# Moving the shared expert's products to other steps of a batch in an attention and mixture-of-experts kernel

## The chip, the cores and the metric

One NeuronCore of a Trainium2 chip (trn2). The metric is the device time of one execution of the kernel, in microseconds (us); smaller is better. The kernel before was timed three times.

## What is computed

The input x has 8 batches of 512 rows of 256 numbers. Cut to what matters:

```
xn = layernorm(x)                                  # over the 256 columns
q, k, v = xn @ qkv_w.T                             # 32 heads of width 8
p = softmax(where(|distance| in window 8, q.k * scale * mask, -inf))
s = (p @ v) @ proj_w.T + proj_b                    # local attention
e, score = argmax(xn @ router_w), sigmoid(max(xn @ router_w))     # one of 8 experts a row
routed = (silu(xs @ gate_w[e]) * (xs @ up_w[e])) @ down_w[e]      # xs = xn * score
shared = (silu(xn @ shared_gate_w) * (xn @ shared_up_w)) @ shared_down_w
out = x + s * silu(routed + shared)
```

## The kernel before, in words

The attention is cut into U = 64 steps of two blocks of 32 query rows, UB = 8 steps to a batch. Each engine has its own program, and each program is a loop `for n in range(LAST + 1)` (67 steps, 0 to 66) in which every other piece of work has been given a step by hand. The functions that say what stands in a step are `jobs_of(n)` (products of TensorE that pass through the psM banks), `silu_at(n)` and `result_at(n)`.

Attention in step n: TensorE makes the scores of n into psS (L939, L943). VectorE scales them into Sx (L719, "weigh") and takes row maxima (L729, "largest"); GpSimd adds the band mask in some steps (L439) and subtracts the maxima (L445); ScalarE takes exp (L508) one step later; VectorE transposes the weights in that step (L751, "flipped"); two steps after the scores TensorE multiplies them with the values into psV (L968, "weighted"), and VectorE divides by the sums (L759, L771) and turns the result (L780). L968 of step n waits for VectorE's division in its step n-1; VectorE's division in step n waits for L968 of step n.

The psM jobs. There are four psM banks; `ORDER` lists all jobs, a job's bank is its place in the list modulo 4, and TensorE waits before a job until the job four places ahead of it has been read out (`bank`, `freed`). The jobs, with their lines on TensorE:

- `q`, `k0` in steps 0 and 4 of a batch and `k1` in steps 1 and 5 (L918, L923), of the next half batch; ScalarE copies them out (L497 for q, L478 for k), into qBD and kBD;
- `tp` (L908, transposes of the rows of the next batch) and `v` (L954, four value and router products at the end of the step), in steps 1 to 7 only; ScalarE copies both out (L478, to xnT and to vS); `v` waits for the copies to xnT;
- `sg`, `su`, `sd`, the shared expert: for a batch `sg, su, sg, su, sd, sd`, in steps 0, 1, 2, 3, 4 and 5. `sg` and `su` are L995, and `sd` L990. After sg ScalarE takes tanh (L524) and VectorE makes ag (L787); after su VectorE makes hTs (L792); sd is copied out by ScalarE (L478);
- `xa`, `xb`, `xc`, the routed experts, in pairs in steps 18 to 39 (L1009, L1018, L1027): the rows are transposed, multiplied by gate and up weights, then by down weights. ScalarE takes a tanh of xb (L538), VectorE gates it (L736, L743, ehT), ScalarE copies xc out (L478 to yb) and stores it;
- `pr`, the output projection (L976), in even steps from 4; VectorE adds the bias (L798).

Around them: VectorE normalises the rows of batch n + 1 in step n (L654) for n below 7, keeps the router's values (L660, `logits`), which waits for the four `v` of the step, and after step 7's chooses experts and ranks rows in steps 7 to 10 (L666 to L710). GpSimd then scatters the 32 row tiles, five to a step from step 10 (L424), each after ScalarE has scaled the tile (L576). When all are in DRAM, SyncE loads expert rows (L361) and weights (L348), and the pairs begin in step 18. From step 40 the results are put together, for 16 groups c of two row tiles: in step `silu_at(c) - 1` GpSimd gathers the routed rows on top of the shared ones (L455), in step `silu_at(c)` ScalarE waits for that DMA and takes tanh (L553, ahead of the step's k, q and shared work on its queue) and VectorE multiplies (L804), and in step `result_at(c)` VectorE makes the product with the attention (L811), which GpSimd adds to the output (L432).

Order within a step where it matters below. TensorE: scores, q/k, tp, xc, xb (first), L968, xb (second), xa (first), the shared product, xa (second), v, pr. VectorE: weigh, largest (after flipped in masked steps), normalise, flipped, division, turn, the shared work, silu, logits, attention, result. ScalarE: exp, silu, q/k copies, tp copies, row scaling, xc, xb, xa, the shared work, xa, v.

```
    if n < U and n % UB < 6 and n != U - 3:
        found.append((("sg", "su", "sg", "su", "sd", "sd")[n % UB], n))
```

Of the kernel before, what the change touches and what calls it, by code (L numbers as in the profile page):

```python
# [16 lines left out]
BATCH, SEQ, C = 8, 512, 256  # L17
# [16 lines left out]
U = NTOK // (2 * QB)  # L34
UB = SEQ // (2 * QB)
# [12 lines left out]
BT = SEQ // P  # L48
# [10 lines left out]
NC = T // CT  # L59
LAST = U + 2  # L60
C_STEP = E0 + NP + 2

C_ID = 0
C_M = C_ID + P
# [49 lines left out]
def pair_at(n, lag):  # L114
    p = n - E0 - lag
    return [i for i in (2 * p, 2 * p + 1) if 0 <= i < NX]


def jobs_of(n):

    if n == -1:
        return [("tp", 0), ("tp", 1), ("q", 0), ("k0", 0), ("k1", 0)] + [("v", t) for t in range(BT)]
    found = []
    h = n // UH + 1
    if h < NH and n % UH == 0:
        found += [("q", h), ("k0", h)]
    if h < NH and n % UH == 1:
        found.append(("k1", h))
    if 1 <= n < BATCH:
        found += [("tp", 2 * n), ("tp", 2 * n + 1)]  # L130
    if n == ROUTE:
        found.append(("cnt", 0))
    found += [("xc", i) for i in pair_at(n, 2)]
    found += [("xb", i) for i in pair_at(n, 1)]
    found += [("xa", i) for i in pair_at(n, 0)[:1]]
    if n < U and n % UB < 6 and n != U - 3:
        found.append((("sg", "su", "sg", "su", "sd", "sd")[n % UB], n))
    if n == U:
        found.append(("sd", U - 3))
    found += [("xa", i) for i in pair_at(n, 0)[1:]]  # L140
    if 1 <= n < BATCH:
        found += [("v", t) for t in range(n * BT, n * BT + BT)]
    if n >= 4 and n % 2 == 0 and (n - 4) // 2 < T:
        found.append(("pr", (n - 4) // 2))
    return found


def silu_at(n):
    last = {NC - 2: U - 1, NC - 1: LAST}
    return [c for c in range(NC) if last.get(c, max(C_STEP + 1 + c * 4 // 3, 2 * BT * (c // 2) + 5 + c % 2)) == n]  # L150


def result_at(n):
    last = {NC - 2: U + 1, NC - 1: LAST + 1}
    return [c for c in range(NC) if last.get(c, max(C_STEP + 2 + c * 4 // 3, 4 * c + 6)) == n]


ORDER = [job for n in range(-1, LAST + 1) for job in jobs_of(n)]
JOB = {job: k for k, job in enumerate(ORDER)}


def build(nc, x, wqkv_d, wproj_d, router_w, gate_w, up_w, down_w, sgate_w, sup_w, sdown_w,
# [3 lines left out]
    with ctx:  # L166
# [100 lines left out]
        def full(eng, job):  # L267
            eng.wait_ge(m_full[JOB[job] % MB], JOB[job] // MB + 1)
            return psM[JOB[job] % MB]
# [30 lines left out]
        def _(sp):  # L300
# [62 lines left out]
            def preset(k):  # L363
                rows = slice(k * NTOK // 8, min((k + 1) * NTOK // 8, NTOK - CT * P))
                sp.dma_start(out[rows, :], x[rows, :]).then_inc(d_pre, 16)

            for n in range(LAST + 1):
                if BATCH < n - 1 < U:
                    spread_v(n - 1)
                if ROUTE <= n < ROUTE + 8:  # L370
                    preset(n - ROUTE)
                if n == C_STEP:
                    full(sp, ("xc", NX - 1))
# [31 lines left out]
        def _(pool):  # L405
# [53 lines left out]
            for n in range(LAST + 1):  # L459
                if n < U:  # L460
                    if masked_late(n):
                        banded(n)
                    subtract(n)
                if n == SENT:
                    pool.wait_ge(s_fill, 16 * 10)
                    pool.wait_ge(r_slot, 1)
                for t in range((n - SENT) * SPS, min((n - SENT + 1) * SPS, T)):
                    if t >= 0:
                        scatter(t)
                for c in silu_at(n + 1):  # L470
                    gather(c)
                for c in result_at(n - 1):
                    add_out(c)

        @block.scalar
        def _(act):
# [101 lines left out]
            for n in range(LAST + 1):  # L578
                if 1 <= n <= U:
                    exps(n - 1)  # L580
                for c in silu_at(n):
                    silu(c)
                for job in jobs_of(n):
                    if job[0] in ("q", "k0", "k1"):
                        qk_out(*job)
                    if job[0] == "tp":
                        rows_of(job[1])
# [15 lines left out]
                for job in jobs_of(n):  # L603
                    if job[0] in ("sg", "sd"):
                        shared(*job)
# [7 lines left out]
        def _(dve):  # L613
# [226 lines left out]
            for n in range(LAST + 1):  # L840
# [34 lines left out]
                for c in silu_at(n):  # L875
                    silu(c)
# [233 lines left out]
```

## Time and profile before

| what | value |
|---|---|
| median of 3 runs | 590.56 us (589.58 to 590.71) |
| the profiled execution | 589.39 us, its span 587.6 us |
| TensorE busy, share of the span | 541.6 us, 92% |
| VectorE | 437.7 us, 74% |
| ScalarE | 240.9 us, 41% |
| GpSimd | 254.1 us, 43% |
| TensorE's mean granted clock | 0.986 of full |

Busy shares are averages over stages in which different engines set the pace. An engine's idle time names in angle brackets who ended it: "[1.07 <-DVE hTs L792]" is 1.07 us of idle time that ended when VectorE's L792 had written hTs. The steps can be told apart in the trace by the first scores (L939 or L943) of each. Names in the rows: PE is TensorE, DVE VectorE, ACT ScalarE, POOL GpSimd, SP SyncE.

### The profile page before, as it was taken

What the parts mean: (1) busy time and instruction counts of PE and PEld (TensorE: products, weight loads), DVE (VectorE), ACT (ScalarE), POOL (GpSimd) and SP (SyncE); (2) the same over time, 40 slices, a digit from 0 to 9 for tenths busy, and PEclk for the clock granted to TensorE, in tenths of its full rate; (3) what the DMA queues carried; (4) which work ended last, traced back from release to release, by engine and by line L of the source; (5) the groups of instructions that cost most, each with busy time, mean ns of one, the idle gap of its engine ahead of it and who ended that gap; (6) DMA issues with size and microseconds to landing.
All of it is one profiled execution on the core that took longest, in us unless ns stands there. A gap on an engine that the chain in (4) does not pass through costs nothing.

```text
span 587.6 us, 10330 instructions
## 1 busy us (share of the span) xinstructions
PE 541.6 (92%) x3302; PEld 468.8 (80%) x3302; DVE 437.7 (74%) x1026; ACT 240.9 (41%) x506; POOL 254.1 (43%) x187
## 2 busy tenths in 40 slices
PE   3979999979988999999999999999999999989872
PEld 2757899758867899988899988899888887868762
DVE  4868668998768556566556656645899999999995
ACT  1562554446652443433443442354434364453120
POOL 5333324148885223322322422222365967877452
PEclk9999999989998999999999999999999999999996
DMA  8725433335525667756566756644233756456323
GB/s 295 235 99 185 138 131 104 94 104 181 162 99 157 209 181 215 219 165 210 170 189 207 209 176 207 205 139 134 57 63 55 108 73 88 73 83 91 56 43 55
DMA packets 106633, 83.17 MB, mean 142 GB/s; under 512 B 42196, under 2 KB 104788, under 8 KB 106452
## 3 DMA queue, kind: packets, MB, share of 16 engines
q1 hardware_dynamic: 90740, 65.07, 37.8%
q0 software_dynamic: 10224, 12.33, 12.6%
q10 hardware_dynamic: 5616, 5.11, 2.5%
q8 instruction: 27, 0.44, 0.3%
q14 instruction: 26, 0.21, 0.1%
HBM read 59.41 MB, written 27.00 MB: 147 GB/s over the span
## 4 chain that ended last, share of the span: by engine, by line
PE 54%; DVE 17%; POOL 11%; issue 5%; DMA 5%; ACT 5%; SPq 1%; ACTq 0%; DVEq 0%
PE psM L1018 11%; PE psV L968 10%; PE psS L943 7%; PE psM L1027 5%; POOL xnT L455 4%; PE psM L995 4%; DMA xnT<-ys_dram,slot 4%; POOL Sx L445 3%; PE psM L954 3%; DVE O L771 3%; PE psM L918 3%; PE psM L990 3%; DVE PTs L751 3%; PE psM L923 2%; PE psM L976 2%
## 5 line engine op out<-in xcount | busy, mean ns | idle before, releaser
L445 POOL TENSOR_TENSOR Sx<-Sx,mx 128x752 f32<-128x752 f32 x64 | 98.9, 1545 | 123.4 <-DVE mx L729 123.0
L968 PE MATMUL psV<-VB,PTs 128*128 128x132 f32 x1024 | 131.2, 280 | 14.8 <-DVE O L771 14.8
L968 PEld LDWEIGHTS psV<-VB,PTs 128*128 128x128 f32 x1024 | 125.3, 190 | 19.9 <-issue 18.6
L439 POOL TENSOR_TENSOR Sx<-Sx,cst 128x752 f32<-128x752 f32 x28 | 47.0, 1678 | 173.2 <-DVE Sx L719 173.2
L943 PE MATMUL psS<-kBD,qBD 128*128 128x188 f32 x512 | 97.8, 323 | 0.2 <-DVE Sx L719 0.2
L943 PEld LDWEIGHTS psS<-kBD,qBD 128*128 128x128 f32 x512 | 84.7, 190 | 9.5 <-issue 2.5
L751 DVE STREAM_TRANSPOSE PTs<-Sx 128x512 f32<-128x512 f32 x128 | 82.8, 685 | 4.2 <-ACT Sx L508 4.1
L719 DVE TENSOR_TENSOR Sx<-psS,cst 128x752 f32<-128x752 f32 x64 | 60.0, 938 | 26.9 <-PE psS L943 26.5
L771 DVE TENSOR_TENSOR O<-psV,rs 32x128 f32<-32x128 f32 x256 | 73.5, 287 | 4.8
L1018 PE MATMUL psM<-xT,EB 128*128 128x128 f32 x624 | 76.5, 276 | 0.2 <-DMA EB<-in_L_ffn_up_w 0.2
L1018 PEld LDWEIGHTS psM<-xT,EB 128*128 128x128 f32 x624 | 73.8, 192 | 2.6 <-ACT qBD L497 1.4
L729 DVE TENSOR_REDUCE mx<-Sx 128x16 f32<-128x752 f32 x64 | 59.6, 931 | 13.0 <-POOL Sx L439 11.8
L508 ACT ACTIVATE Sx<-Sx 128x752 f32<-128x752 f32 x64 | 52.9, 827 | 38.7 <-POOL Sx L445 38.5
L995 PE MATMUL psM<-xnT,wsgu 128*128 128x512 f32 x128 | 61.7, 605 | 2.1 <-DVE ag L787 2.1
L478 ACT ACTIVATE kBD<-psM 32x272 f32<-32x272 f32 x128 | 49.3, 385 | 15.3 <-PE psM L923 14.1
L455 POOL DMA_INDIRECT xnT<-ys_dram,slot x28 | 46.5, 1659 | 9.3 <-issue 6.2
L497 ACT ACTIVATE qBD<-psM,cst 128x512 f32<-128x512 f32 x64 | 38.7, 687 | 22.1 <-PE psM L918 22.1
L538 ACT ACTIVATE et<-psM 128x256 f32<-128x256 f32 x39 | 15.0, 384 | 77.5 <-PE psM L1018 73.9
L736 DVE SCALAR_TENSOR_TENSOR ea<-et,psM 128x256 f32<-128x256 f32 x39 | 16.4, 420 | 37.3 <-ACT et L538 36.2
L995 PEld LDWEIGHTS psM<-xnT,wsgu 128*128 128x128 f32 x128 | 22.6, 196 | 18.5 <-issue 16.2
L1027 PE MATMUL psM<-EB,ehT 128*128 128x256 f32 x156 | 36.9, 379 | 0.0
L976 PE MATMUL psM<-wp,OT 128*128 128x256 f32 x128 | 33.9, 388 | 2.7 <-DVE OT L780 2.0
(111 smaller groups left out, 681.5 us busy)
## 6 DMA issues: line engine op xcount, KB each, us to landing
EB<-in_L_ffn_gate_w SPq DMA_DIRECT2D x39, 256.0 KB, 3.2
EB<-in_L_ffn_up_w SPq DMA_DIRECT2D x39, 256.0 KB, 3.7
EB<-in_L_ffn_down_w SPq DMA_DIRECT2D x39, 256.0 KB, 3.0
VB<-v_dram SPq DMA_DIRECT2D x256, 32.0 KB
stage<-xs_dram SPq DMA_DIRECT2D x39, 128.0 KB, 2.3
ys_dram<-yb ACTq DMA_DIRECT2D x39, 128.0 KB, 3.2
xs_dram<-blank SPq DMA_DIRECT2D x9, 512.0 KB, 3.2
v_dram<-vS SPq DMA_DIRECT2D x8, 512.0 KB, 3.0
```

The lines of the kernel that those rows point to most:

```text
L445: nc.gpsimd.tensor_tensor(s, s, mx[n % 3][:, :].unsqueeze(2).broadcast_to([P, 2 * G, KW]), ALU.subtract).then_inc(a_sub, 1)
L455: pool.indirect_dma_start(shared_rows(c * CT)[:, k, :], None, ys_dram, bass.IndirectOffsetOnAxis(ap=slot[:, t:t + 1], axis=0), compute_op= ...
L508: nc.scalar.activation(s, s, ACT.Exp).then_inc(a_exp, 1)
L719: tt(s, psS[:, :, 0:BW].rearrange("p j (g k) -> p j g k", k=KW), mw.unsqueeze(1).unsqueeze(1).broadcast_to([P, 2, G, KW]), ALU.mult).then_ ...
L729: reduce(mx[n % 3][:, :], Sx[n % 3][:, :, 0:KW], AX, ALU.max).then_inc(a_max, 1)
L751: last = nc.vector.transpose(PTs[n % 2][:, k, :, :, :].rearrange("p j i (r q) -> p (j i r) q", q=QB), Sx[n % 3][:, :, k * QB:(k + 1) * QB])
L771: last = tt(o[rows], v[rows, :, :, HD * h:HD * h + HD], inverse[rows].unsqueeze(3).broadcast_to([QB, KC, 8, HD]), ALU.mult)
L943: last = mm(psS[:, j, i * HS * KW:(i + 1) * HS * KW], qBD[h % 2][:, j, k, :, :].rearrange("p s q -> p (s q)"), kBD[h % 2][:, j, :, k * QB: ...
L968: last = mm(psV[:, j, at:at + HS * VW], PTs[n % 2][:, k, j, i, :], VB[n % 2][:, i, k, :, VW * j:VW * j + VW], start=k == 0, stop=k == 1)
L995: last = mm(ps[:, :], wsgu[:, kc, at:at + P], xnT[:, b, kc, WIN:WIN + SEQ], start=kc == 0, stop=kc == KC - 1)
L1018: last = mm(ps[:, f * P:(f + 1) * P], egu[:, i % 2, kc, f * P:(f + 1) * P], xT[:, i % 2, kc, :], start=kc == 0, stop=kc == KC - 1)
L1027: last = mm(ps[:, 0:C], ehT[:, i % 2, fc, :], edn[:, i % 2, fc, :], start=fc == 0, stop=fc == KC - 1)
```

## The change

The same six products of a batch stand in its steps 1, 2, 3, 5, 6 and 7, in the same order, for batches 0 to 6. In batch 7 all stays. The names of the jobs keep the batch and the place among the six, so all semaphores count as before. In `silu_at` a bound on the step moves by two.

```diff
+SHARED = ("sg", "su", "sg", "su", "sd", "sd")
+SPREAD = (1, 2, 3, 5, 6, 7)
...
-    if n < U and n % UB < 6 and n != U - 3:
-        found.append((("sg", "su", "sg", "su", "sd", "sd")[n % UB], n))
+    b, k = divmod(n, UB)
+    if b < BATCH - 1 and k in SPREAD:
+        k = SPREAD.index(k)
+        found.append((SHARED[k], b * UB + k))
+    if b == BATCH - 1 and k < 5:
+        found.append((SHARED[k], n))
     if n == U:
-        found.append(("sd", U - 3))
+        found.append((SHARED[5], U - 3))
...
-    return [c for c in range(NC) if last.get(c, max(C_STEP + 1 + c * 4 // 3, 2 * BT * (c // 2) + 5 + c % 2)) == n]
+    return [c for c in range(NC) if last.get(c, max(C_STEP + 1 + c * 4 // 3, 2 * BT * (c // 2) + 7 + c % 2)) == n]
```

## Rows read from the trace of the kernel before

**Rows 1.** Windows by stage: start:end, length, then each engine's busy time

```profile
core 0: us, PE busy (x) PEld busy (x) DVE busy (x) ACT busy (x) POOL busy (x), PEclk, DMA share, GB/s
22.09:101.62 79.53, 73.22 (x401) 61.51 (x400) 58.99 (x136) 38.14 (x79) 25.43 (x16) 1.00 0.40 131
127.85:186.62 58.77, 54.34 (x304) 45.00 (x303) 45.95 (x109) 32.44 (x67) 44.57 (x41) 0.97 0.48 149
186.62:425.71 239.09, 238.40 (x1605) 216.74 (x1605) 148.01 (x339) 93.28 (x216) 65.77 (x43) 1.00 0.62 181
425.71:576.28 150.57, 140.22 (x839) 118.28 (x837) 140.41 (x315) 56.48 (x102) 101.69 (x68) 1.00 0.49 73
```

**Rows 2.** Windows of single steps: 2, 4, 5, 6 and 7

```profile
41.44:52.03 10.59, 9.53 (x53) 7.69 (x52) 8.11 (x17) 3.97 (x8) 3.20 (x2) 1.00 0.48 162
62.64:75.47 12.83, 12.83 (x74) 11.46 (x73) 7.60 (x17) 8.47 (x18) 3.20 (x2) 1.00 0.40 134
75.47:85.66 10.19, 10.19 (x61) 9.26 (x60) 7.66 (x16) 4.86 (x11) 3.19 (x2) 1.00 0.47 156
85.66:94.07 8.41, 8.41 (x53) 7.77 (x52) 7.04 (x15) 3.76 (x8) 3.01 (x2) 1.00 0.26 79
94.07:101.62 7.55, 7.55 (x49) 6.92 (x48) 5.60 (x15) 3.09 (x6) 3.30 (x3) 1.00 0.49 158
```

**Rows 3.** Timeline of steps 0 and 1, single engines: start us, us, what

```profile
31.52 1.28 ACT L524 ACT_TABLE_LOAD   x1
32.81 0.60 ACT L524 ACTIVATE tg<-psM 128x512 f32<-128x512 f32 x1
...
33.52 0.69 DVE L787 SCALAR_TENSOR_TENSOR ag<-tg,psM 128x512 f32<-128x512 f32 x1 [2.14 <-ACT tg L524]
...
36.86 2.91 PE L954 MATMUL psM<-wqkv,xnT 128*128 128x264 f32 x12 [0.61 <-ACT xnT L478]
40.45 1.16 PE L954 MATMUL psM<-wqkv,xnT 128*128 128x264 f32 x4 [0.68 <-DVE hTs L792]
```

**Rows 4.** Timeline of step 4: ScalarE's last row copies, TensorE's sd and first v

```profile
69.74 1.09 ACT L478 ACTIVATE xnT<-psM 128x512 f32<-128x512 f32 x2
...
69.28 1.89 PE L990 MATMUL psM<-wsdn,hTs 128*128 128x256 f32 x8
71.00 1.32 PE L954 MATMUL psM<-wqkv,xnT 128*128 128x264 f32 x5
```

**Rows 5.** Timeline, VectorE: it takes step 7's router values

```profile
102.25 0.18 DVE L660 COPY EB<-vS 128x32 f32<-128x32 f32 x1 [1.29 <-ACT vS L478]
```

**Rows 6.** Waits of GpSimd from 127.85 to 178.1: total us, times, longest

```profile
POOL xs_dram L424 <- issue: 6.4, 24, 0.3
```

**Rows 7.** Timeline, TensorE: the first expert product, step 19

```profile
186.62 0.57 PE L1018 MATMUL psM<-xT,EB 128*128 128x128 f32 x3 [0.25 <-DMA EB<-in_L_ffn_up_w]
```

**Rows 8.** Windows of single steps with experts: 24 (sg), 28 (sd), 32 (sg)

```profile
238.55:253.04 14.49, 14.48 (x90) 12.35 (x89) 7.72 (x18) 8.22 (x20) 3.11 (x2) 1.00 0.70 200
286.53:300.75 14.22, 14.22 (x94) 13.08 (x93) 7.09 (x16) 7.63 (x18) 3.11 (x2) 1.00 0.64 181
330.81:345.96 15.15, 14.48 (x90) 12.35 (x89) 7.86 (x18) 8.65 (x20) 3.11 (x2) 1.00 0.72 215
```

**Rows 9.** Waits of VectorE from 427.6 to 576: total us, times, longest

```profile
DVE ag L787 <- ACT tg L524: 0.9, 2, 0.5
DVE xnT L804 <- ACT EB L553: 0.9, 1, 0.9
```

**Rows 10.** Timeline of steps 46 and 49, VectorE and ScalarE

```profile
459.47 0.94 DVE L719 TENSOR_TENSOR Sx<-psS,cst 128x752 f32<-128x752 f32 x1 [0.65 <-PE psS L943]
...
482.15 1.57 ACT L478 ACTIVATE kBD<-psM 32x272 f32<-32x272 f32 x4
...
483.59 0.69 DVE L792 SCALAR_TENSOR_TENSOR hTs<-ag,psM 128x512 f32<-128x512 f32 x1
484.19 0.68 DVE L804 SCALAR_TENSOR_TENSOR xnT<-EB,xnT 128x512 f32<-128x512 f32 x1
```

## The prediction

> **What bounds the kernel now.** I first cut the span into stages, because the 92% of TensorE is an average [rows 1]. From the first expert product to step 41 TensorE is busy 238.40 of 239.09 us: there it is the bound, and a product placed there costs its full time. From step 41 on VectorE is busy 140.41 of 150.57 us, with TensorE at 140.22; the waits tell who sets the pace: after 427.6 VectorE waits 1.8 us for ScalarE [rows 9] and 0.65 us for TensorE [rows 10], and what is left of its 10 idle us lies in pauses too short for the view of waits, between instructions that depend on each other. So VectorE bounds that stage. In between, from 127.85 to 178.1, GpSimd scatters; its pauses are 24 of at most 0.3 us [rows 6], so the scatter runs at its own speed and whatever the others do is hidden. Before that, steps 4 to 7 are TensorE's (busy 12.83 of 12.83, 10.19 of 10.19, 8.41 of 8.41, 7.55 of 7.55), and step 2 is not (9.53 of 10.59) [rows 2]. There TensorE's fourth `v` waits until VectorE has read the shared product out of its bank (the wait of 0.68 us for hTs in step 1 is of this kind [rows 3]).
>
> So the change moves products between stages of different owners. No instruction is added or removed, no DMA moves to another place of a queue, and silu_at returns the same steps: for c = 12 the larger term is 57 against 53 before and 55 now, for c = 13 it is 58 against 54 and 56. Only places count.
>
> **Prices.** A shared product takes TensorE 1.72 us, from the start of sd to that of the next job [rows 4]. Its VectorE part takes 0.60 us, from start to start [rows 10].
>
> **Batch 0.** Step 0 loses its sg. VectorE had waited 2.14 us there for the tanh, which came after a table load of 1.28 us [rows 3]. Now VectorE goes on with step 1 2.7 us earlier (the wait and the product). ScalarE, though, needs the load all the same, now ahead of the first exp; exp, k copies and row copies follow without the tanh's 0.5 us ahead of them, of which exp can use 0.3, since it waits for the subtracted maxima. So the first `v`, which waited for these copies until 36.86, comes 0.3 us earlier. The last `v` waited 0.68 us for hTs and started at 40.45 [rows 3]; ag is ready by then, as VectorE is early. With 3.6 us for four `v` from 36.55 the step ends at 40.15 instead of 41.44: **-1.3 us**.
>
> The row shows that the tanh starts 0.01 us after the load ends. The Trainium skill ("ScalarE: Activation LUTs", "What ACT_TABLE_LOAD costs") says otherwise: 1.28 us for the load and another 1.38 us for a drain. By that rule exp and the copies behind it would come 1.4 us later and this gain would be gone; by the row it stands, and the sum takes the row.
>
> Steps 2 and 3 keep a sg or su, and their 10.6 us. Step 4 loses sd, 1.72 us of a full step. But its `v` need the row copies, which ScalarE ends at 70.83, behind the q and k copies; sd ended, and `v` began, at 71.00 [rows 4]. sd filled a wait: its removal gives **0.0** (-0.1 to 0; with the wait gone it would be -1.7). Step 5 trades sd for su; now its last `v` waits for hTs as in step 2, so it takes 10.6 instead of 10.19: **+0.4**. Steps 6 and 7 get sd, while TensorE is full and the row copies are early: **+1.7** each. Sum of batch 0: -1.3 + 0.4 + 1.7 + 1.7 = **+2.5 us**, at the moment when VectorE takes the last router values, for which it waits at 102.25 [rows 5].
>
> **Routing and scatter.** From there to the first scatter VectorE runs without a pause. Step 8 loses its ag: **-0.6**; step 9 has ag for hTs. GpSimd starts 1.9 us later and ends 1.9 us later. Batch 1's and half of batch 2's products lie beside the scatter: 0. The first expert product waits for its weights, which are loaded after the last scatter [rows 7]: it too is 1.9 us later. Putting sd into steps 14 and 15 is covered by GpSimd, whose span there has TensorE idle for 4.4 us [rows 1]; if that cover is gone it costs 1.7 a piece.
>
> **Experts, to step 41.** Before, the products of steps 19, 20, 21, 24 to 29, 32 to 37 and 40 fall in it: 16. After: 19, 21, 22, 23, 25, 26, 27, 29, 30, 31, 33, 34, 35, 37, 38, 39: 16. Equal. What changes is one wait. Steps 24 and 32 took 14.49 and 15.15 against 14.22 of step 28 with the same kinds of work [rows 8]; in both the preceding step was short (no shared product in step 7 of a batch), and `pr` waited for the gating of the second xb, whose bank it takes over. Without sg in the step `pr` takes the bank of the first xb, and the preceding step has an sd more. **-1.2** (0.27 + 0.93). Step 40 is reached 0.5 us later, step 41 1.2 us earlier, both on top of the 1.9.
>
> **Results.** Here VectorE's queue is the sum. Gathers stand with the older steps, so ScalarE's silu ends its DMA wait when it did. Behind it on ScalarE's queue stand k1 and then tanh, and sg now stands in steps 41 and 49 beside a k1, where su stood, which needs no ScalarE. In step 41 ag waits some 0.4. In step 45 hTs comes in (+0.6), while the wait of 0.65 us in step 46 for scores [rows 10] goes, as TensorE lost a product in step 44. In step 48 ag goes (-0.6). In step 49 the k copies end at 483.7 [rows 10] and tanh takes 0.6 more, so ag starts near 484.3 less the 0.9 that all has come forward, about 483.5, where hTs stood: the 1.5 us gained by then are all lost. In step 50 there is no tanh to wait for: -0.4 to -0.5 of the 0.9 [rows 9]. In step 53 hTs comes in (+0.6), hidden in the 0.9 us wait for the gathered rows [rows 9]. From step 41 to the end: what was -1.2 becomes **-0.5**.
>
> Total: +1.9 - 0.5 = **+1.4 us**. Against the profiled execution's own 589.39 that is 590.8; that execution is 1.2 under the median of 590.56, so the forecast for the median is **592.0**. A measurement of this kernel can tell about 0.2%, 1.2 us, from no change, that is, above 591.7 or below 589.4.
>
> **Rivals.**
> - *The front gain is not there* (0.18): the table load runs only once the maxima are subtracted, or the copies wait otherwise. For it: the load now stands between k0's copy and exp on the path to the first `v`. Against it: the load of [rows 3] began as soon as ScalarE was free. +1.3: 593.3. A drain as the Trainium skill has it (same page and section) would cost the same.
> - *Less is lost in the results* (0.25): the tanh waits in steps 41 and 49 do not arise, or half of sd in steps 6 and 7 finds cover; then 1.4 less: 590.6, no change.
> - *Slots are filled evenly and TensorE profits* (0.12), the faster side: if in batches 5 and 6 TensorE, not VectorE, set the pace, the short steps 6 and 7 would take up products for nothing. TensorE is idle for 10.4 us of that stage [rows 1]; batch 7 and the end, whose order stays, hold the larger part, so I take 4 for the two batches. Then 592.0 - 4 = 588. It decides if VectorE has pauses of over half a microsecond in most steps of batches 5 and 6; rows 9 show two or three in all, so it is unlikely.
> - *It does not do what it says*: the order is computed, and the job counts agree; nothing left for it.
>
> **How the numbers follow.** My case has 0.45, from 591.4 to 592.6, of which a third lies under the bound of 591.7. Slower: 0.30 + 0.18 + 0.03 from the upper end of the second rival = 0.51. Same: 0.15 + 0.22 from the second rival = 0.37. Faster: 0.12. The range 589.8 to 594.0 leaves out the faster rival and reaches over the front one.
>
> **What would show it.** Step 2 starts near 40.1; step 4 still takes 12.8 us, with TensorE idle 1.7 us before `v`; step 5 takes 10.6, steps 6 and 7 10.1 and 9.3; the router values come at 104.8; the first scatter and the first expert product come 1.9 us later; steps with q among the experts take 12.5 us and none waits at L976; ag waits for tanh in steps 41 and 49. It is wrong if steps 6 and 7 stay short, if step 4 shrinks, or if GpSimd has longer pauses between scatters.

## The result, and the profile after

Median of the changed kernel 594.49 us (592.32 to 597.88, 7 runs), against 590.56 for the kernel before in the same comparison: ratio 1.0091, 95% interval 1.0075 to 1.0108. It is slower, as forecast, but by 3.9 us where 1.4 stood, and outside the range of 589.8 to 594.0. The profiled execution took 597.88 us, the longest of the seven, with a span of 596.0 and a mean granted clock of 0.980; the kernel before had 589.39, 587.6 and 0.986. The profiled execution is thus 3.4 us over the median, and its mean clock is the lowest of the seven, so its trace shows more time at half clock than most executions had. The seven times go with that clock: 592.32 and 593.21 at 0.992 and 0.990, 594.35 to 594.79 at 0.988 to 0.984, 597.72 and 597.88 at 0.980.

In the changed kernel the lines behind the diff are 6 higher (L960 is the `v` of L954 before, L1001 the sg and su, L530 the tanh, L793 ag). Windows by stage, as in [rows 1]; the first is steps 0 to 7, the third from just before the first expert product (192.84) to step 41, the fourth the results:

```profile
core 0: us, PE busy (x) PEld busy (x) DVE busy (x) ACT busy (x) POOL busy (x), PEclk, DMA share, GB/s
22.20:107.38 85.18, 76.31 (x402) 63.63 (x401) 59.60 (x137) 38.11 (x79) 25.36 (x16) 0.96 0.37 122
...
192.68:432.31 239.63, 239.47 (x1604) 218.30 (x1605) 146.20 (x335) 92.42 (x214) 64.08 (x42) 0.99 0.62 181
432.31:584.93 152.62, 142.31 (x843) 118.72 (x841) 141.54 (x320) 58.13 (x105) 102.49 (x69) 1.00 0.50 73
```

Steps 0 to 7 grew from 79.5 to 85.2 us, and their clock is no longer full. The expert stretch kept its length (0.4 us longer, counted from the first product) although two waits went, since its clock is 0.99. The results grew by 2.1. Single windows of the same trace, as in [rows 2, 8]: a stretch of step 1, then steps 4, 5, 6, 7, 24, 28 and 32:

```profile
35.90:42.70 6.80, 5.94 (x14) 4.58 (x15) 2.20 (x4) 2.27 (x6) 1.45 (x1) 0.50 0.01 2
...
64.54:77.36 12.82, 11.30 (x66) 10.09 (x65) 7.60 (x17) 7.86 (x17) 3.20 (x2) 1.00 0.40 134
77.36:87.96 10.60, 10.44 (x57) 8.41 (x56) 8.37 (x17) 4.25 (x10) 3.21 (x2) 1.00 0.46 150
87.96:98.10 10.14, 10.14 (x61) 9.29 (x60) 7.61 (x17) 4.63 (x10) 3.20 (x2) 1.00 0.21 65
98.10:107.38 9.28, 9.28 (x58) 8.44 (x57) 5.16 (x12) 3.30 (x7) 3.12 (x2) 1.00 0.40 127
248.10:260.60 12.50, 12.50 (x87) 11.61 (x86) 5.59 (x14) 7.66 (x18) 3.11 (x2) 1.00 0.56 169
294.08:306.58 12.50, 12.50 (x87) 11.61 (x86) 6.63 (x15) 7.65 (x18) 3.10 (x2) 1.00 0.57 170
340.08:352.57 12.49, 12.49 (x86) 11.61 (x85) 5.73 (x14) 7.65 (x18) 3.11 (x2) 1.00 0.56 165
```

Every step length at full clock is the forecast one: 12.8, 10.6, 10.1, 9.3, and 12.5 for the expert steps with a q. Step 1 is not. Its timeline on TensorE, and the first expert product:

```profile
31.67 1.98 PE L1001 MATMUL psM<-xnT,wsgu 128*128 128x512 f32 x4 [0.23 <-ACT kBD L484]
36.76 6.74 PE L960 MATMUL psM<-wqkv,xnT 128*128 128x264 f32 x16 [3.11 <-ACT xnT L484]
...
192.84 3.65 PE L1024 MATMUL psM<-xT,EB 128*128 128x128 f32 x16 [2.00 <-DMA EB<-in_L_ffn_up_w]
196.32 2.00 PE L974 MATMUL psV<-VB,PTs 128*128 128x132 f32 x16
```

The four `v` start at 36.76, as before [rows 3], but take 6.74 us: from 35.9 to 42.7 the granted clock is 0.50, the 1.2 GHz level, and step 2 starts at 43.33 where 40.15 was forecast. TensorE had been idle for 2.2 us when the clock fell. Without an sg in step 0 the product of step 1 no longer waits for VectorE: it starts at 31.67 where su stood at 34.26, and TensorE's idle time, 3.11 us of it, now lies in one piece right ahead of `v`. The first expert product shows it again: 3.65 us, where the second such product in the same trace, at full clock, takes 1.95.

### The profile page after: what moved, and what is told of

Its sections match the earlier page's. It is cut to its first block, busy times and chain, and to the rows that moved or that the text cites. A ratio compares the mean times of both kernels' runs of the same rounds, so it can differ in the third digit from the quotient of the medians.

```text
span 596.0 us, 10330 instructions
## 1 busy us (share of the span) xinstructions
PE 544.7 (91%) x3302; PEld 472.2 (79%) x3302; DVE 438.7 (74%) x1026; ACT 241.0 (40%) x506; POOL 253.8 (43%) x187
## 3 DMA queue, kind: packets, MB, share of 16 engines
q0 software_dynamic: 10224, 12.33, 12.5%
## 4 chain that ended last, share of the span: by engine, by line
PE 49%; DVE 21%; POOL 9%; issue 8%; ACT 5%; DMA 5%; SPq 1%; DVEq 0%; ACTq 0%; POOLq 0%
PE psM L1024 12%; PE psV L974 8%; PE psS L949 6%; PE psM L1033 6%; PE psM L960 4%; DVE O L777 4%; DVE PTs L757 4%; PE psM L1001 3%; DVE Sx L725 3%; POOL Sx L451 3%; DMA xnT<-ys_dram,slot 3%; PE psM L924 2%; POOL xs_dram L430 2%; POOL xnT L461 2%; PE psM L996 2%
## 5 line engine op out<-in xcount | busy, mean ns | idle before, releaser
L974 PE MATMUL psV<-VB,PTs 128*128 128x132 f32 x1024 | 132.8, 282 | 19.7 <-DVE O L777 17.6
L1024 PE MATMUL psM<-xT,EB 128*128 128x128 f32 x624 | 78.1, 279 | 2.0 <-DMA EB<-in_L_ffn_up_w 2.0
L1024 PEld LDWEIGHTS psM<-xT,EB 128*128 128x128 f32 x624 | 75.4, 195 | 4.3 <-issue 2.3
L1001 PE MATMUL psM<-xnT,wsgu 128*128 128x512 f32 x128 | 60.2, 593 | 0.2 <-ACT kBD L484 0.2
L484 ACT ACTIVATE kBD<-psM 32x272 f32<-32x272 f32 x128 | 49.3, 385 | 14.6 <-PE psM L929 13.3
L960 PE MATMUL psM<-wqkv,xnT 128*128 128x264 f32 x128 | 34.3, 419 | 7.7 <-ACT xnT L484 4.6
L960 PEld LDWEIGHTS psM<-wqkv,xnT 128*128 128x128 f32 x128 | 25.6, 205 | 16.8 <-issue 7.0
```

Source lines behind the costliest of these rows:

```text
L960: last = mm(ps[:, 0:VE], xnT[:, b, kc, at:at + P], wqkv[:, kc, 2 * C:3 * C + E], start=kc == 0, stop=kc == KC - 1)
L974: last = mm(psV[:, j, at:at + HS * VW], PTs[n % 2][:, k, j, i, :], VB[n % 2][:, i, k, :, VW * j:VW * j + VW], start=k == 0, stop=k == 1)
L1001: last = mm(ps[:, :], wsgu[:, kc, at:at + P], xnT[:, b, kc, WIN:WIN + SEQ], start=kc == 0, stop=kc == KC - 1)
L1024: last = mm(ps[:, f * P:(f + 1) * P], egu[:, i % 2, kc, f * P:(f + 1) * P], xT[:, i % 2, kc, :], start=kc == 0, stop=kc == KC - 1)
```

## The experiments

Each was timed in five rounds against the kernel before on the same chip; the medians of that one are 589.50 for e1 to e4, 589.77 for e5 to e8 and 590.14 for e9 and e10. In their traces lines are 14 higher than in the kernel before (`v` is L968, the scores L957, ag L801). The steps of the six products are written out by batch:

```diff
-    if b < BATCH - 1 and k in SPREAD:
-        k = SPREAD.index(k)
+    if b < BATCH - 1 and k in PLACES[b]:
+        k = PLACES[b].index(k)
         found.append((SHARED[k], b * UB + k))
```

**e1_again**: all of PLACES is (1, 2, 3, 5, 6, 7), the changed kernel.

> The changed kernel once more, the places written out batch by batch. Theory A (TensorE's clock): the 3.9 us by which the changed kernel is slower are the 1.4 of the forecast plus stretches at half clock that the kernel before does not have, near 36 us (step 1) and near 193 us (start of the expert products). Then the trace again shows a granted clock of half in step 1, four value products that take about 6.7 us instead of 3.6, step 2 starting near 43.3 us, and the times again scatter by several us, the lower ones with the higher mean clock. Rival B (my sizes were wrong at full clock): step 2 starts late with the clock at full. Time 592 to 598, median near 594.5.

Measured: 593.66 us (593.09 to 597.38), ratio 1.0070 (1.0052 to 1.0088). The trace shows the half clock in step 1 again, here from 37.7 to 41.1, so that `v` takes 5.49 us, and again at the start of the expert products. Theory A holds in kind: the half clock is there again, for 3.4 us where the changed kernel's trace had 6.8. In size it is a miss here, with `v` at 5.49 us and step 2 at 42.11 where 6.7 and 43.3 were expected.

**e2_batch0_only** puts batches 1 to 6 back to their old places, **e3_batch0_stays** batch 0 alone; the latter against e1_again:

```diff
 PLACES = (
-    (1, 2, 3, 5, 6, 7),
+    (0, 1, 2, 3, 4, 5),
     (1, 2, 3, 5, 6, 7),
...
```

> Only batch 0 has its products in steps 1, 2, 3, 5, 6, 7; batches 1 to 6 as before. Theory A: the router values come 2.5 us later than before at full clock and 5.8 us later with the half clock of step 1, and nothing after it gives that back, so 593 to 596 us, that is 2.5 to 5.8 us slower than before. Rival C (the loss is made in the later batches): within 1 us of before.

> Batch 0 as before, batches 1 to 6 moved. Theory A: step 8 loses its ag (-0.6), the experts lose two waits (-1.2), the results give back 1.9 by the trace of the changed kernel, and a second half clock at the start of the expert products costs 0 to 2.7: 590.7 to 593.4 us, 0 to 2.8 slower than before. Rival C: 3 us or more slower than before, nearly all of the loss.

Measured: e2 594.31 us, ratio 1.0092 (1.0070 to 1.0115); e3 590.78, ratio 1.0021 (1.0007 to 1.0036). Batch 0 alone makes a loss as large as the whole change's; the other six together cost 1.3 us. Rival C is out. The two parts, 4.8 and 1.3 us, add up to more than the 4.2 of e1_again; e2 has only five times, two of them at 596.0, and no run shows more of why.

**e4_filled**: seven products in step 1 that nobody reads.

```diff
                     if n < U and job[0] in ("sg", "su", "sd"):
                         shared(*job)
+                if n == 1:
+                    for _ in range(7):
+                        mm(psV[:, 0, 0:C], wqkv[:, 0, 0:P], wqkv[:, 0, 0:C], start=True, stop=True)
```

> The changed kernel with seven more products of 256 columns in step 1, behind the shared product, into psV, which nothing has used by then; they fill the 3.1 us that TensorE waits for the row copies, and their result is never read. Theory A: the granted clock stays full in step 1, the four value products take 3.6 to 3.8 us, step 2 starts near 40.2 to 40.6 instead of 43.3, the median is about 3 us under that of the changed kernel where that one has the half clock (near 592) and the times scatter less. Rival B: step 2 starts at 43.3 or later all the same and the time is that of the changed kernel.

Measured: 592.22 us (591.58 to 593.42), ratio 1.0044 (1.0028 to 1.0061): more work, 1.4 us less than e1_again. The intervals of the two ratios overlap, but of e4's seven times, 591.58 to 593.42, six lie under the shortest of e1_again, 593.09. Its timeline on TensorE in step 1 and the window that was at half clock:

```profile
33.67 3.19 PE L1081 MATMUL psV<-wqkv 128*128 128x256 f32 x14
36.94 3.80 PE L968 MATMUL psM<-wqkv,xnT 128*128 128x264 f32 x16
40.58 1.44 PE L957 MATMUL psS<-kBD,qBD 128*128 128x188 f32 x8
...
35.90:42.70 6.80, 6.71 (x37) 5.75 (x36) 3.23 (x6) 3.88 (x9) 1.45 (x1) 1.00 0.08 30
```

The clock stays at 1.00, `v` takes 3.80 us in place of 6.74, and step 2 starts at 40.58: the forecast's 40.15, 0.3 for a later start of the loop (step 0 at 22.37 against 22.09), and 0.15. The filling itself costs nothing: `v` starts 14.6 us after step 0 in e4 and in e1. From step 0 to step 2 e4 takes 18.2 us, e1 19.9 and the kernel before 19.35, so the gain of the forecast is there as soon as the clock is full. That the half clock made the loss of step 1 is shown, and a longer chain is out. That TensorE's idle time brings it on rests on this one trace at full clock beside four without filling that are not, and on the narrower times. The gain is under the 3 us expected, since the half clock of step 1, which costs 2.9 us in the changed kernel's trace, costs 1.7 in the others: `v` took 5.5 us in the traces of e1, e2 and e10.

**e10_batch0_early**: only batch 0 moved, to (1, 2, 3, 4, 5, 6).

> Only batch 0 moved, into its steps 1, 2, 3, 4, 5 and 6 in place of 1, 2, 3, 5, 6 and 7. Theory A: a product in step 4 costs nothing, since TensorE would wait there for the row copies; step 5 takes 10.2 again instead of 10.6 and step 7 its old 7.55 instead of 9.28. So the router values come 2.1 us earlier than in e2_batch0_only (at full clock 0.4 us later than before, with the half clock of step 1 up to 3.6): 2.1 us faster than e2, about 592. Rival H (a product costs 1.7 wherever it stands in batch 0): the same time as e2 within 0.5 us, step 4 takes 14.5.

Measured: 591.34 us, ratio 1.0030 (1.0014 to 1.0045). Each against the kernel before of its own comparison, e2 is 4.8 us slower and e10 1.2. Windows of steps 4 to 7, first of e2, then of e10:

```profile
63.37:76.18 12.81, 11.29 (x65) 10.08 (x64) 7.61 (x17) 7.85 (x17) 3.20 (x2) 1.00 0.41 134
76.18:86.78 10.60, 10.45 (x57) 8.41 (x56) 8.36 (x17) 4.26 (x10) 3.20 (x2) 1.00 0.46 150
...
96.92:106.19 9.27, 9.27 (x57) 8.44 (x56) 5.16 (x12) 3.30 (x7) 3.12 (x2) 1.00 0.43 129
```

```profile
63.38:76.20 12.82, 12.82 (x70) 10.69 (x69) 8.30 (x18) 7.87 (x17) 3.20 (x2) 1.00 0.41 134
76.20:86.39 10.19, 10.19 (x61) 9.26 (x60) 7.66 (x16) 4.86 (x11) 3.19 (x2) 1.00 0.47 156
...
96.53:104.08 7.55, 7.55 (x50) 6.92 (x49) 5.16 (x12) 2.71 (x6) 3.11 (x2) 1.00 0.51 158
```

Step 4 takes 12.8 us with a product (TensorE busy for all of it) and without (11.29): its product is free. Steps 5 and 7 are 0.4 and 1.7 shorter, 2.1 in all, and in the traces step 8 starts at 104.08 against 106.19. The medians are 3.6 apart, 1.5 more than that; e2's is a median of five times between 593.33 and 596.0, and what makes the rest is not shown. Rival H is out: step 4 did not grow.

**e5_experts_only**: only batches 3 and 4 moved.

> Only batches 3 and 4 moved, which lie wholly beside the expert products. Theory A: the number of shared products in the stretch that TensorE bounds stays 16; steps 24 and 32 lose their wait, so step 41 starts 1.2 us earlier than before and nothing behind it changes: 1.2 us faster than before. Rival D (evening out gives more, or the waits come back elsewhere in the expert steps): over 2 us faster, or no change, with step 41 not 1.2 us earlier.

Measured: 588.50 us, ratio 0.998 (0.997 to 0.999), 1.3 us faster, as Theory A has it. Steps 24, 28 and 32 all take 12.50 us, TensorE never waits between 200 and 420, and step 41 starts at 424.71 against 425.71. The two waits of [rows 8] were real and are all that spreading brings there.

**e8_batches_1_2**: only batches 1 and 2 moved.

> Only batches 1 and 2 moved. Theory A: the scatter starts 0.6 us earlier (ag of step 8), steps 22 and 23 get a product of 1.7 us more than steps 16, 18 and 20 give up, 0.3 comes back from the wait of step 24, and a half clock at the start of the expert products may cost up to 1.8: 0.8 to 2.6 us slower than before. Rival G (the scatter hides these moves): within 0.5 us of before.

Measured: 591.04 us, ratio 1.0025 (1.0012 to 1.0037), 1.3 us slower, within what was expected. In its trace the first subtraction ahead of the scatter is 0.45 us earlier than before and step 41 is 1.0 us later: the product too many in steps 22 and 23.

**e7_batches_3_to_6** puts batches 0 to 2 back to their old places; **e6_sg_clear_of_k1** has batch 6 in another order as well, so that its sg do not meet a k1 or a silu on ScalarE's queue. e6 against e7:

```diff
 PLACES = (
...
     (1, 2, 3, 5, 6, 7),
-    (1, 2, 3, 5, 6, 7),
+    (0, 1, 4, 5, 6, 7),
 )
```

> Batches 0 to 2 as before, 3 to 6 moved as in the change. Theory A: step 41 starts 2.9 us earlier (1.2 for the two waits, 1.7 because step 40 loses a product that TensorE bounds and no other step of that stretch gets one), and from step 41 on VectorE loses 2.1 us, as in the changed kernel: 0.8 us faster than before. Rival F (the loss of the change lies in these batches): 1 us or more slower than before.

> Batches 0 to 2 as before, 3 to 5 moved as in the change, batch 6 in its steps 0, 1, 4, 5, 6 and 7, so that none of its sg stands beside a k1 or a silu. Theory A: as e7, but without the wait of about 2 us for the tanh in step 49; ag of step 48 comes back with 0.6: 1.0 to 1.5 us faster than e7, 1.8 to 2.3 us faster than before. Rival E (the gathers, not the tanh, hold VectorE back there): the same as e7 within 0.5 us, with longer waits for the silu.

Measured: e7 589.10 us, ratio 0.9982 (0.9971 to 0.9993), 0.7 faster where 0.8 was expected; e6 586.70, ratio 0.9943 (0.9925 to 0.9960), 2.4 us under e7 where 1.0 to 1.5 was expected. VectorE's waits in the results, first of the changed kernel from 434.2 on, then of e7, then of e6 (total us, times, longest):

```profile
DVE ag L793 <- ACT tg L530: 3.0, 3, 1.9
DVE xnT L810 <- ACT EB L559: 0.7, 1, 0.7
DVE OT L786 <- DVE O L777: 0.5, 1, 0.5
```

```profile
DVE ag L801 <- ACT tg L538: 2.8, 3, 1.9
DVE xnT L818 <- ACT EB L567: 1.7, 2, 1.1
DVE OT L794 <- DVE O L785: 0.5, 1, 0.5
```

```profile
DVE ag L801 <- ACT tg L538: 0.8, 2, 0.5
DVE xnT L818 <- ACT EB L567: 0.4, 2, 0.3
```

With both sg of batch 6 in steps without a silu, the tanh waits fall from 2.8 to 0.8, and the waits for gathered rows fall with them. So the tanh of step 49 was the head of it; rival E, by which the waits for the silu would have grown, is out. Its own wait was 1.93 us; e6 moves both sg and an su at once, and how the rest of the 2.4 divides among them was not taken apart. How it comes about in the changed kernel, ScalarE's timeline and VectorE's ag in step 49:

```profile
489.47 0.63 ACT L559 ACTIVATE EB<-xnT 128x512 f32<-128x512 f32 x1 [5.33 <-DMA xnT<-ys_dram,slot]
490.12 1.59 ACT L484 ACTIVATE kBD<-psM 32x272 f32<-32x272 f32 x4
491.73 0.60 ACT L530 ACTIVATE tg<-psM 128x512 f32<-128x512 f32 x1
...
492.43 0.69 DVE L793 SCALAR_TENSOR_TENSOR ag<-tg,psM 128x512 f32<-128x512 f32 x1 [1.85 <-ACT tg L530]
```

The tanh stands behind the silu, which waits for a DMA, and behind the four copies of k1, and VectorE, the bound, stands still for 1.85 us.

**e9_best**: e6 with batch 1 moved too; batches 0, 2 and 7 keep their places.

> e6 with batch 1 moved too. Theory A: all of batch 1's products stay beside the scatter, and step 8 has no ag, so the scatter and all behind it come 0.6 us earlier: 3.5 us faster than before, 0.6 faster than e6 (586 us). Rival G (more idle time of TensorE at the routing costs half clock on the path): 1 to 2 us slower than e6.

Measured: 585.58 us (584.95 to 587.58), ratio 0.9935 (0.9912 to 0.9959), the fastest of all: 4.6 us under the kernel before where 3.5 was expected, and 1.1 under e6. Rival G is out. In its trace step 41 starts 3.2 us earlier than before.

## Why the prediction was right in sign and wrong in size

**Batch 0, steps 2 to 7: right.** 12.8, 10.6, 10.1 and 9.3 us, sd in step 4 filling a wait (TensorE idle 1.5 us there without it), the two sd in steps 6 and 7 paid in full: 64.05 us for steps 2 to 7 against 60.18, +3.9 where +3.8 was forecast.

**Batch 0, steps 0 and 1: the step that failed.** "With 3.6 us for four `v` from 36.55 the step ends at 40.15 instead of 41.44: -1.3 us." The waits were nearly right: counted from step 0, `v` starts 0.2 us earlier (0.3 was forecast), and VectorE no longer waits there. The price of `v` was that of a full clock. In all four traces with batch 0 moved and nothing filled in the clock was halved in step 1: `v` took 5.5 or 6.7 us, and steps 0 and 1 together 19.9 or 21.1 against 19.35. The term is +0.5 to +1.8, not -1.3. The forecast does not speak of TensorE's clock at all. The rival of a missing front gain comes nearer in time, 593.3, by another cause.

The half clock is not new with the change, though. In four of the seven traces with batch 0 in its old places (e5, e6, e7 and e8; not before, e3 and e9) step 1 has 3.4 us of it too. TensorE in e7, and the window at half clock:

```profile
34.15 2.65 PE L1009 MATMUL psM<-xnT,wsgu 128*128 128x512 f32 x4 [2.06 <-DVE ag L801]
36.74 4.79 PE L968 MATMUL psM<-wqkv,xnT 128*128 128x264 f32 x16
35.34:38.75 3.41, 3.41 (x7) 1.63 (x6) 3.41 (x6) 1.23 (x3) 1.51 (x1) 0.50 0.02 5
```

There the su takes 2.65 us for 1.98, and yet steps 0 and 1 last 19.4 us, as at full clock (19.7 in e5, the most of the four): the last `v` would have waited 0.68 us for hTs anyway [rows 3], and `v` for the copies 0.6. The change took these waits away, and with them the cover; now the half clock is paid in full. Whether the move also makes it more frequent, four traces of four against four of seven do not tell.

The table load behaved as the row of before had it. ScalarE's timeline in the changed kernel:

```profile
31.63 1.28 ACT L514 ACT_TABLE_LOAD   x1
33.06 0.83 ACT L514 ACTIVATE Sx<-Sx 128x752 f32<-128x752 f32 x1
```

exp starts 0.15 us after the load ends, as soon as the maxima are subtracted. The Trainium skill's further 1.38 us of drain ("ScalarE: Activation LUTs", "What ACT_TABLE_LOAD costs") does not show in either trace, so the 593.3 that goes with it would have been nearer the measured time for a wrong reason.

**Routing and scatter: right.** GpSimd's pauses stay at 0.3 us or less, and ag leaves 0.6: the router values came 5.75 us later than before in the trace, the subtraction ahead of the scatter 5.15.

**Start of the experts: a term left at nothing.** In the traces of the change and of e1 the clock was halved once more as the expert products begin; from the first one to step 20 it costs 1.4 to 1.6 us. It shows in none of the other traces, so it comes in some executions only. In the two traces that have it the wait for weights ahead of the first product was 2.0 and 2.6 us, against 0.25 before [rows 7], and the product came 1.1 and 1.3 us later after the start of the scatter. A wait of 1.5 to 1.7 us in e3, e5, e6 and e9 brought no half clock. Why the weights come late in some executions stays open.

**Experts: right.** Step 41 is 1.23 us nearer to step 20 than before, 1.2 was forecast; e5 shows this gain alone, 1.1 in its trace and 1.3 by the medians.

**Results: right mechanisms, one size too small.** "What was -1.2 becomes -0.5" should have read +0.9: in the changed kernel and in e1, e3 and e4 the stage lost 1.9 to 2.6 us (3.0 in e7), where 0.7 was forecast. The wait in step 41 (0.56 for 0.4), hTs in step 45 against the wait in 46, and ag of step 48 are as forecast. The size that failed is "about 483.5, where hTs stood". Counted from step 20 (194.27 before, 202.10 now), the silu ahead of that tanh starts behind its DMA wait when it did before (287.4 us against 287.3), as the forecast itself says; but the forecast then takes 0.9 off the k copies and the tanh behind it, as if they had come forward with VectorE. They had not: ag starts 290.3 us after step 20, 1.0 later than hTs did, and VectorE waits 1.85 to 2.0 us for it. A wait of 0.5 us ahead of VectorE's turn in step 52 was not in the sum either. The two make up the 1.4 us that were missing. Waits of 0.2 to 0.7 us for gathered rows shortly before step 49 were not forecast; they only take from the wait for the tanh.

**The sum.** At full clock the forecast's mechanisms give 1.4 + 1.3 (results) = 2.7, and e4_filled measured 2.7 by the medians (3.3 in its trace). The half clock of step 1 is what lies between e4 and e1: 1.4 us by the medians, 1.7 in steps 0 and 1 of the traces. The profiled execution of the changed kernel is 8.5 us longer than that of the kernel before, 7.1 more than forecast: 3.1 of them lie in steps 0 and 1, 2.7 around the first expert product (1.1 ahead of it, 1.6 behind) and 1.2 from step 41 to the end. The range was too narrow because the clock and the start of the experts were given no width.

The faster rival had no ground as it was put: the stage grew by 2.1 us when its products were spread, with VectorE waiting for the tanh. Yet some moves do bring time, for other reasons: fewer products where TensorE is the bound (e7), and a free VectorE (e6).

## What to carry to other kernels

Moving work within a written-out order is worth what its old and its new place are worth: read for each step who bounds it, and price every product at its new place; the moves here held a gain of 1.3 us (e5) and losses of 1.7 a piece side by side, and sorting them, with another order for batch 6, gave 4.6 us. Evening out the number of products is no aim in itself. Before work is taken out of a stretch where TensorE already waits, look at how long it will then be idle and what it runs next: at half clock the price of the work behind it nearly doubled here. Look also at which waits go with the work: a wait can hide a slow clock, as in e5 to e8, and a kernel that loses the wait pays for what was there all along. And on a shared queue ask what stands ahead: a short tanh behind a DMA wait held the engine that mattered.

## What the runs showed of the hardware

Filling TensorE's idle time with 3.2 us of useless products made the program 1.4 us faster by the medians and kept its times within 1.8 us instead of 4.3 (seven each). The granted clock fell to 0.50 in step 1 in eight of eleven traces without filling, and cost 1.7 to 2.9 us in the four with batch 0 moved, 0.3 or less in the four with batch 0 in its old places. The same program's times differed by 5.6 us with the mean granted clock (0.992 to 0.980), while those of the kernel before, in the first comparison, lay within 1.9.
